# A Mamba-2 layer with a low-rank feed-forward: three convolutions moved ahead of a barrier, and the last tiles of the tail reordered

## What is computed

```python
proj = x_norm @ in_proj_w.T                  # 512 -> gate 8192, conv input 8192 + 2*8*128, dt 128
hBC  = silu(causal depthwise conv of 4 taps over the conv input + conv_b)
hs, Bm, Cm = hBC split into 128 heads x 64, 8 groups x 128, 8 groups x 128
dt = clip(softplus(dt + dt_bias), 0, 100);  A_dt = -exp(A_log) * dt, cumulated in chunks of 128 tokens
Y  = (C B^T * decay inside the chunk) @ (hs*dt) + C @ (state carried from earlier chunks) + hs * D
g  = Y * silu(gate), normed over each group of 1024 features, * norm_w
x  = x + g @ out_proj_w.T
h  = layernorm(x);  out = x + h @ W.T + b + sum over 16 experts of probs_e * (h @ A_e.T) @ B_e.T
```

## Time and profile before

| | us |
|---|---|
| median of 3 runs | 1635.05 (1633.94 to 1636.73) |
| the profiled execution | 1639.27 |
| its span, first to last instruction | 1637.5 |
| PE busy | 1598.2 |
| VectorE, ScalarE, GpSimd busy | 1261.2, 1147.9, 711.3 |
| mean granted clock of TensorE | 0.991 |

### The profile page before, as it was taken

The page is one execution under the profiler, slowest core; times in us unless marked ns, Lnnn a source line. Parts: engine busy times, 40 slices in busy tenths (PEclk is TensorE's granted clock), DMA queues, the critical chain, the costliest instruction groups (busy, mean ns, idle before and its releaser), DMA issues.

```text
span 1637.5 us, 26761 instructions
## 1 busy us (share of the span) xinstructions
PE 1598.2 (98%) x9616; PEld 1357.8 (83%) x9616; DVE 1261.2 (77%) x1974; ACT 1147.9 (70%) x2002; POOL 711.3 (43%) x543
## 2 busy tenths in 40 slices
PE   7799999999999999999999999999999999999997
PEld 4678888888888888888888888888888888888876
DVE  6577777887778787787778877787877877787776
ACT  5398668776777767876787766777678767777741
POOL 1145445354443543454453544435444444434542
PEclk9799999999999999999999999999999999999999
DMA  5533233323232332332333232233223323233211
GB/s 200 186 111 106 78 110 99 102 84 120 87 97 95 110 97 85 114 103 77 111 98 103 84 120 88 86 106 110 90 92 114 102 77 112 93 108 94 75 43 52
DMA packets 88244, 164.56 MB, mean 100 GB/s; under 512 B 23344, under 2 KB 39728, under 8 KB 87856
## 3 DMA queue, kind: packets, MB, share of 16 engines
q1 hardware_dynamic: 88112, 162.85, 30.5%
HBM read 157.03 MB, written 5.77 MB: 99 GB/s over the span
## 4 chain that ended last, share of the span: by engine, by line
PE 90%; issue 2%; DVE 2%; POOL 1%; ACT 1%; DVEq 0%; POOLq 0%; ACTq 0%
PE g_bank L714 9%; PE g_bank L715 8%; PE g_bank L716 8%; PE d_bank L733 7%; PE x_bank L714 7%; PE x_bank L715 7%; PE x_bank L716 7%; PE d_bank L773 3%; PE d_bank L775 3%; PE d_bank L774 3%; PE x_bank L773 3%; PE x_bank L774 3%; PE x_bank L775 3%; PE state_bank L722 2%; PE state_bank L740 2%; PE turn_bank L740 2%
## 5 line engine op out<-in xcount | busy, mean ns | idle before, releaser
L1294 POOL TENSOR_TENSOR w_low<-raw,w_high 128x512 fp32r<-128x512 f32 x141 | 182.3, 1293 | 580.2 <-ACT w_high L915 580.2
L1068 DVE SCALAR_TENSOR_TENSOR hs<-x_bank,cols,hs 128x1022 f32<-128x1022 f32 (+2 forms) x192 | 245.4, 1278 | 98.5 <-ACT hs L935 96.2
L925 ACT ACTIVATE scores<-scores,tables 128x128 f32<-128x128 f32 x1024 | 312.4, 392 | 0.0
L1308 POOL TENSOR_TENSOR y<-y,gate 128x512 f32<-128x512 f32 x128 | 188.7, 1494 | 205.5 <-DVE y L1130 205.5
L935 ACT ACTIVATE hs<-x_bank,cols 128x1024 f32<-128x1024 f32 x64 | 77.0, 1203 | 278.3 <-PE x_bank L716 278.3
L714 PE MATMUL g_bank<-x_high,w_high 128*128 128x512 f32 x624 | 251.2, 403 | 1.3 <-DVE bc L1147 1.3
L715 PE MATMUL g_bank<-x_low,w_high 128*128 128x512 f32 x624 | 244.0, 391 | 0.0
L716 PE MATMUL g_bank<-x_high,w_low 128*128 128x512 f32 x624 | 243.7, 391 | 0.0
L714 PE MATMUL x_bank<-x_high,w_high 128*128 128x512 f32 x512 | 199.6, 390 | 0.5 <-PEq L146 0.5
L716 PE MATMUL x_bank<-x_high,w_low 128*128 128x512 f32 x512 | 199.2, 389 | 0.0
L715 PE MATMUL x_bank<-x_low,w_high 128*128 128x512 f32 x512 | 199.2, 389 | 0.0
(11 more groups left out here) (185 smaller groups left out, 3492.2 us busy)
## 6 DMA issues: line engine op xcount, KB each, us to landing
scores<-sums_dram SPq DMA_DIRECT2D x128, 512.0 KB, 4.9
raw<-w_in SPq DMA_DIRECT2D x144, 256.0 KB, 2.9
grown_rows<-grown_dram SPq DMA_DIRECT2D x256, 96.0 KB, 2.8
out_raw<-w_out SPq DMA_DIRECT2D x64, 256.0 KB, 3.5
xt<-x SPq DMA_DIRECT2D x8, 256.0 KB, 5.6
mixed<-x SPq DMA_DIRECT2D x1, 2048.0 KB, 12.2
out<-mixed SPq DMA_DIRECT2D x8, 256.0 KB, 2.0
table_dram<-table SPq DMA_DIRECT2D x2, 768.0 KB, 3.2
```

The costliest lines, as they stand in the source:

```text
L925: op = s.activation(at, at, ACT.Relu, bias=col[:, r, c:c + 1], scale=-1.0)
L1068: v.scalar_tensor_tensor(out=hs[:, q % 2, :, i:], in0=x_bank[:, :, 0:SEQ - i], scalar=cols[:, q, TAPS - 1 - i:TAPS - i], in1=hs[:, q % 2, ...
L1294: pool.tensor_tensor(w_low[:, slot], raw[:, slot], w_high[:, slot].bitcast(F32), ALU.subtract)\
L1308: pool.tensor_tensor(y[:, b], y[:, b], gate[:, q % 2, b], ALU.mult).then_inc(y_ready, 1)
```

## The change

- In the prologue, PE projects B, C and now also the first x tile (into `head_bank`, `g_bank` and `x_bank`), straight after the dt product; the low-rank products come last, two banks by turns. ScalarE makes the first tap of all three and copies the six tables out of PSUM and the low-rank products to SBUF; VectorE makes the three other taps of all three and copies no table; GpSimd splits two more weight tiles and adds the low-rank products to the dense weight.
- SP loads `mixed` after the weight tiles, stores the dense weight last, and issues the loads of the first scores and growths ahead of the barrier. The load of the first tables waits for its own stores alone.
- Behind the barrier PE begins with the gate tile; B-C products go to `d_bank`; hs is turned between the two halves of the next x tile. ScalarE does the three silus first, and its differences (Relu) are split from its exponentials (`differences`, `decays`).
- In every unit, VectorE's `score` of sequence 0 comes ahead of the addition of output bank 3.
- In the tail, tile 8 is multiplied half by half (`out_part`), tile 9 after the sum of squares, the norm goes by pairs of tiles, the products use four banks and the splits three slots.

```diff
--- before.py
+++ after.py
...
-            sp.dma_start(mixed[:], x_tokens).then_inc(mixed_in, 16)
...
-            sp.wait_ge(dense_ready, KT)
-            sp.dma_start(dense_dram, dense[:].rearrange("p k d -> p (k d)")).then_inc(dense_stored, 16)
...
-                sp.dma_start(chunk_by_head[b], chunk_decay[:, b]).then_inc(stored[b], 16)
+                sp.dma_start(chunk_by_head[b], chunk_decay[:, b]).then_inc(tables_stored[b], 16)
+            for b in range(BATCH):
+                sp.wait_ge(sums_stored[b], 16)
+                sp.dma_start(scores[:, 0, b].rearrange("p r c l -> p (r c l)"),
+                             sums_dram[b * ALL].partition_broadcast(P)).then_inc(sums_in[0][b], 16)
+            for b in range(BATCH):
                 sp.wait_ge(table_ready, 3 * (b + 1))
                 sp.dma_start(table_dram[b].rearrange("p g n -> p (g n)"),
                              table[:, b].rearrange("p g k n -> p (g k n)"))\
-                  .then_inc(stored[b], 16)
+                  .then_inc(tables_stored[b], 16)
+            for b in range(BATCH):
+                sp.dma_start(scores[:, 1, b].rearrange("p r c l -> p (r c l)"),
+                             sums_dram[b * ALL + 1].partition_broadcast(P)).then_inc(sums_in[1][b], 16)
+            for b in range(BATCH):
+                sp.wait_ge(grown_stored[b], 16)
+                rows = grown_dram[b * ALL].rearrange("(r n) -> r n", r=PAIR)
+                for r in range(PAIR):
+                    sp.dma_start(grown_rows[r * HEAD_DIM:(r + 1) * HEAD_DIM, b].rearrange("p c l -> p (c l)"),
+                                 rows[r, P:].partition_broadcast(HEAD_DIM)).then_inc(grown_in[b], 16)
+            sp.wait_ge(dense_ready, KT)
+            sp.dma_start(dense_dram, dense[:].rearrange("p k d -> p (k d)")).then_inc(dense_stored, 16)
...
+            pool.wait_ge(wd_in, 16)
+            for k in range(KT):
+                pool.wait_ge(lora_out, k + 1)
+                pool.tensor_tensor(dense[:, k], dense[:, k], wd[:, k], ALU.add).then_inc(dense_ready, 1)
...
+                pe.wait_ge(bc_conv_ready, 1)
+                reached(pe, lora_out, k - 1)
...
+            for t in (0, 1):
+                for b in range(BATCH):
+                    project(t, b)
+            pe.wait_ge(z_ready, BATCH)
+            turn_table(0)
+            for b in range(BATCH):
+                project(2, b)
+            for i in range(1, 6):
+                turn_table(i)
             pe.wait_ge(lora_ready, ER)
             for k in range(KT):
                 lora(k)
-            pe.wait_ge(z_ready, BATCH)
-            project(0, 0)
-            project(0, 1)
-            turn_table(0)
-            turn_table(1)
-            project(1, 0)
-            for i in range(2, 6):
-                turn_table(i)
-            project(1, 1)
...
+            s.wait_ge(tap_bc_in, 16)
+            bc_tap0(0, head_bank[:])
+            high_part(3)
+            s.wait_ge(lora_in, 48)
+            for r in range(ER):
+                s.activation(lb[:, r], lb[:, r], ACT.Copy, scale=pr[:, r:r + 1]).then_inc(lora_ready, 1)
+            bc_tap0(1, g_bank[:])
+            high_part(4)
+            table_of(0)
+            growth(0)
+            growth(1)
+            for i in range(1, 6):
+                table_of(i)
+            s.wait_ge(cols_in[0], 16)
+            s.wait_ge(projected, BATCH * 3)
+            s.activation(hs[:, 0], x_bank[:], ACT.Identity, scale=cols[:, 0, TAPS - 1:TAPS],
+                         bias=cols[:, 0, TAPS:TAPS + 1]).then_inc(tap0_ready, 1)
+            for k in range(KT):
+                s.wait_ge(lora_product, k + 1)
+                s.activation(dense[:, k], head_bank[:, k % 2], ACT.Copy).then_inc(lora_out, 1)
+
         @block.vector
         def _(v):
             def stats_of(tb):
...
+                bc_tap(i, 0, head_bank)
+            for i in range(1, TAPS):
+                bc_tap(i, 1, g_bank)
+            for i in range(1, TAPS):
+                tap(i)
...
-            sp.wait_ge(dense_stored, 16)
-            for b in range(BATCH):
                 load_tables(0, b, 0)
-                load_sums(0, 0, b)
             load_weight(0, place(0, 2))
             load_out(0, 0)
-            for b in range(BATCH):
-                load_grown(0, b)
-            for b in range(BATCH):
-                load_sums(1, 1, b)
...
+            def out_part(j, c, i):
+                b, q, at = j % 2, flushed(j)[i], slice(c * P, (c + 1) * P)
+                pe.matmul(out_bank[c], y_high[:, q, b, at], out_high[:, q], start=(i == 0), stop=False)
+                pe.matmul(out_bank[c], y_high[:, q, b, at], out_low[:, q], start=False, stop=False)
+                return pe.matmul(out_bank[c], y_low[:, q, b, at], out_high[:, q], start=False, stop=(i == 1))
...
+                if tb in (2, 3):
+                    pe.wait_ge(added, emptied(ALL + 1, tb - 2))
+                if tb >= len(product_bank):
+                    pe.wait_ge(ready, tb + 1 - len(product_bank))
...
+                            if k == 0 and b == 0:
+                                pe.wait_ge(b_tok_ready, 1)
+                                turn_hs(0, 0, 0)
+                                turn_hs(0, 0, 1)
...
-            pe.wait_ge(bc_conv_ready, 1)
+            pe.wait_ge(bc_conv_ready, 2)
             for b in range(BATCH):
-                project(0, 0, b, x_bank[:, b])
+                project(0, 1, b, g_bank[:, b])
...
+                bc_of(b, d_bank)
 
             over_groups(pe, body)
-            later_outs(UNITS + 1, ALL + 1)
+            later_outs(UNITS - 1, ALL - 1)
+
+            pe.wait_ge(out_low_ready, ALL)
+            for c in range(CHUNKS):
+                pe.wait_ge(added, emptied(ALL - 1, c))
+                out_part(UNITS, c, 0)
+            pe.wait_ge(y_low_ready, ALL)
+            for c in range(CHUNKS):
+                out_part(UNITS, c, 1).then_inc(out_done, 1)
+            pe.wait_ge(square_added, (UNITS - 1) * GROUPS)
+            var_of()
+            for c in range(CHUNKS):
+                pe.wait_ge(added, emptied(ALL, c))
+                out_product(UNITS + 1, c)
 
...
-            high_part(0, 1)
-            s.wait_ge(projected, BATCH * 2)
-            s.activation(bc_conv[:, 1], g_bank[:], ACT.Identity, scale=tap_bc[:, 1, TAPS - 1:TAPS],
-                         bias=tap_bc[:, 1, TAPS:TAPS + 1]).then_inc(bc_tap0_ready, 1)
-            high_part(0, 2)
             silu_bc(0, 0)
+            silu_bc(0, 1)
+            silu_hs(0, 0)
+            high_part(0, 3)
+            differences(0, 0, 0, 0)
+            keep_b(0, heads)
             for b in range(BATCH):
+                silu_gate(0, 0, 0, b)
+            differences(0, 0, 0, 1)
+            for b in range(BATCH):
+                decays(0, 0, b)
+            for b in range(BATCH):
+                s.wait_ge(sums_stored[b], 16)
+                s.wait_ge(grown_stored[b], 16)
                 s.wait_ge(tables_stored[b], TABLE_STORES)
             s.wait_ge(dense_stored, 16)
-            keep_b(0, d_bank)
-            tap0(0, 0, 0)
-            high_part(0, 3)
-            silu_bc(0, 1)
-            silu_hs(0, 0)
-            for b in range(BATCH):
-                silu_gate(0, 0, 0, b)
-            for b in range(BATCH):
-                decays(0, 0, 0, b)
...
-            norm_std(0)
             for tb in range(TB):
-                if tb == 3:
-                    norm_std(1)
+                if tb % 2 == 0:
+                    norm_std(tb // 2)
                 s.wait_ge(xt_turned, tb + 1)
-                if tb >= 2:
-                    s.wait_ge(product, tb - 1)
-                s.activation(xt_high[:, tb % 2].rearrange("p k t -> p (k t)"), xn_bank[tb % 2], ACT.Copy)\
+                if tb >= SPLIT:
+                    s.wait_ge(product, tb + 1 - SPLIT)
...
+                    scores_here = last or j not in (5, 6)
+                    if scores_here:
+                        score(g, j, k, 0)
                     if k > 2:
                         add_outs(g, j - 1, (3,))
-                    if last or j not in (5, 6):
-                        for b in range(BATCH):
-                            score(g, j, k, b)
+                    if scores_here:
+                        score(g, j, k, 1)
...
-            for at in range(CHUNKS):
-                normed_out(GROUPS, at)
+
+            def summed(pair):
+                for tb in (2 * pair, 2 * pair + 1):
+                    normed_out(GROUPS, tb)
+
+            summed(0)
             norm_stats(0)
-            norm_stats_end(0)
+            norm_moments(0)
+            summed(1)
+            norm_rstd(0)
             normed(0)
             normed(1)
-            add_outs(GROUPS - 1, UNITS + 1, range(CHUNKS))
-            for at in range(CHUNKS, TB):
-                normed_out(GROUPS, at)
+            norm_stats(1)
             low_of(0)
+            norm_moments(1)
             low_of(1)
+            norm_rstd(1)
             normed(2)
```

(36 more changed lines are left out.)

276 lines of the change are left out of this document (126 added, 150 removed).

## The result

The changed kernel takes **1619.43 us** (median, 1618.50 to 1619.84), the kernel before on the same chip 1635.89 (1633.94 to 1637.21): a ratio of 0.990, 95% interval 0.9887 to 0.9912. That is 16.5 us by the medians, where 22.1 were forecast. The time lies in the range, 6.4 us above the forecast of 1613.0. The profiled execution took 1619.32 (span 1617.6), so this one stands at its median, while the one of before stood 3.4 above the median of 1635.89. Between the two profiled spans lie 19.9 us. In the later comparisons the kernel before had medians of 1636.7 to 1637.9. The changed kernel has no second time of its own; its nearest variants, runs 3 and 4, took 1619.0 and 1618.9 beside 1636.85, so the gain is 16.5 to 18 us.

The account below looks back on a forecast made before the run. PE was taken as the bound, busy 98% of the span with a full middle, so only the ends give time: 14.2 at the start plus 7.9 at the end, 22.1 off 1635.05, gives 1613.0 us; range 1608.5 to 1621.

Parts of the forecast that it names:

- R1: Rival, start: PE's clock falls under lora and at the barrier, tables come late; start gives 9.9, time 1617; chance 0.20.
- R2: Rival, tail: VectorE's sums double beside GpSimd's bias additions, first product at half clock; end gives 3.3, time 1617.5; chance 0.12.
- The 14.2: Start: PE reaches the gate projection of unit 1 at 76.5 in place of 90.70, 14.2 us earlier.
- 58.3: End of the prologue: the barrier falls at about 58.3 us, 1.8 later than before.
- Unseen 1: At the barrier: PE's clock may fall behind a 2.5 us gap; taken as none, 1.9 at the bad end.
- Unseen 2: Behind the barrier: first table load queues behind the dense store; worst 1.2 late, 0.4 past cover; taken as nothing.
- 7.9: Tail: 6.8 earlier, plus 1.9 for a full clock, less 0.8 for VectorE late twice; 7.9 us gained.
- (a): VectorE's score of batch 0 ahead of the fourth output addition: worth 0.6 at unit 63, nothing elsewhere.
- (b): Tail: tile 8 by halves, the half with unit 62 filling PE's wait for y_low; worth 0.6.
- (c): Tail: norm by pairs of tiles, first product 6.8 earlier, PE's gap 1.4 instead of 4.98, clock staying full.
- R3: Rival, middle units: the score swap makes scores end late under GpSimd's work, kernel slower, 1640 at 0.45 per unit; chance 0.03.
- R4: Rival, first units: the freed time turns into waits paced by ScalarE, no gain, 1635; chance 0.03.

Follow-up runs that it names:

- run 3: Changed kernel with VectorE's fourth output addition put back ahead of both scores (no swap): 1619.02 us, ratio to the kernel before 0.9888.
- run 4: Changed kernel plus eleven products that nobody reads, keeping PE busy up to the barrier: 1618.89 us, ratio to the kernel before 0.9886.
- run 1: The kernel before, unchanged, profiled once more: ratio 1.0004; the profiled execution took 1635.38 us.
- run 5: Changed kernel with GpSimd's two later weight splits (tiles 3 and 4) held until VectorE has both sums: 1616.38 us, ratio to the kernel before 0.9879.
- run 9: Changed kernel, y_low of unit 62 behind unit 63's states, additions of banks 2 and 3 ahead of the last y_low: 1617.53 us, ratio 0.9880.
- run 6: Changed kernel with ScalarE's six table copies written contiguously, table entries permuted: 1619.26 us, ratio to the kernel before 0.9896.
- run 2: Kernel before with only the new tail (halves, pairs) and the score swap, old start: 1629.71 us, ratio to the kernel before 0.9955.
- run 7: Changed kernel with the six table copies made by VectorE between its taps instead of ScalarE: 1622.94 us, ratio to the kernel before 0.9920.
- run 8: Changed kernel with VectorE's y_low of unit 62 moved behind the states of unit 63: 1618.78 us, ratio to the kernel before 0.9891.
- run 10: Changed kernel with the edits of run 5 and run 9 together: 1615.14 us, ratio to the kernel before 0.9869.
- run 11: The kernel of run 10 plus products that nobody reads, keeping PE busy up to the barrier: 1614.75 us, ratio to the kernel before 0.9859.

## Why the forecast was right in kind and too good in size

The measured 1619.43 lies in the whole range of 1608.5 to 1621, but above the forecast's own 1609 to 1616.5 and above what R1 or R2 alone would give (1617, 1617.5). It is inside by the bad end alone.

**The step that failed first** is the sentence "I subtract from both". The forecast compared its steps with one profiled execution of before, took the 4.2 us over the median for something that the changed kernel would share, and took it off the sum again. It was not shared. In run 1 the gate of unit 1 is 3.9 earlier and the span 3.8 shorter: 2.3 of it by the end of the dt product, which came early in the changed kernel too, and 1.6 in the very stretch that the change rebuilds. Another part was no excess at all, as later medians of before lie 1.7 to 2.8 us over the 1635.05 that the forecast had. The 14.2 was worked out against 90.70, where 86.80 and 87.08 also occur; nothing let it stand beside a subtraction of the whole 4.2. Of the miss of 6.4 us, 4.2 are this step and 2.2 the terms: 1.4 at the start and 0.7 at the end.

**The rows.** The forecast says that the high waits, 5.0 and 4.6, are all of the end, and puts the 4.6 at unit 63. Its rows don't place them: 1.5 of the 4.6 were at unit 0. The view's highest wait, 9.2 for the normed tiles at the very start, it passes over. A turn with 0.45 to the next instruction took 0.35 at the place named (1612.29 to 1612.64). None of the three moves the sum by more than 0.2.

**Barrier, "58.3".** Right (PE at 58.60, the first issue of SyncE behind it at 58.41), but the working was wrong twice, with errors that cancelled. VectorE had the dt product 1.6 earlier (26.2, not 27.8: the clock had risen sooner), and lost 2.2 us in its two groups to GpSimd's moved splits, (2.39 - 1.29) + (2.42 - 1.36). The forecast priced the splits' move at nothing and had R2's rule only for the tail. The Trainium skill ("SBUF — State Buffer", "Who interferes with whom") says that a VectorE instruction with two SBUF inputs contends with a GpSimd one that reads SBUF; runs 3, 5 and 9 agree. The table copies took 0.98, near the 1.05 taken. By the Trainium skill's rule that each access that crosses to a new 16-byte line pays a penalty ("SBUF — State Buffer", "Door 1: The DMA port swizzle") ScalarE pays for the pattern; the 0.98 with it and the 0.53 of a contiguous copy in run 6 (1.05 for two) agree. The other half of the step, a barrier 1.2 earlier without the pattern, is near the 1.0 of run 6, but was worth no time.

**Behind the barrier.** Unseen 1, the clock, taken as none "because 2.5 is nearer 1.88": the gap was 2.95, and the fall came, for 1.6 of its 1.9. PE's turns of B started at 65.76, where B+5.8 gives 64.1. From there to the gate PE gained 0.3 on the forecast, and 1.4 stayed. Unseen 2, the late tables, came with 1.19, its worst value, and cost nothing more only because PE was late by the clock anyway; in run 4, with a full clock, they did cost. Both had been put side by side as separate bad ends; together they cost the larger, not the sum. The rest of the schedule is right within that 0.3: from the B-C products to the gate of unit 1 it said 11.8 and took 11.5.

**End, "7.9".** 7.2 in the profile, and the same in run 2. The 0.7 that lacks is all in the last stretch, 29.7 from the first product in place of 28.9, and it is its two waits. As idle time they are 0.69 and 0.33, but from start to start, which is what PE loses, they cost 1.5 in place of 0.8: from turn 5 to product 4 pass 1.30 where 0.36 is usual, and from product 4's last matmul to turn 6 0.72 where 0.23 is. Of the 0.7 more, 0.5 is the last pair of sums (1.91 for 1.40), which stands right ahead of the low part of product 4. Part (a), the swap at 0.6, gave its 0.6 and kept 0.4 (run 3). Parts (b) and (c) stood: the gap of 4.98 became 1.13, the first product runs at full clock, product 4 waits 0.69 (0.2 foretold) and turn 6 0.33 (0.6 foretold).

**Rivals.** Of R1's three parts two came, the clock at the barrier and the tables; under lora the clock did not fall (granted 1.00 from 44 to 56 us in the changed kernel, as in its variants of the table below but run 7, where PE waited up to 1.4 for each copy). R2 came as 0.5 in the last pair of sums, which PE paid at product 4. That pair took 0.95 a sum, over the 0.75 that the forecast gave as a sign of being wrong; run 9, with both sums of the first pair stretched, shows that more of it was near. R3 failed as the middle is full, 1400.00 of 1400.00, and no longer than before. R4 failed with at least 8.9 at the start.

**Still open:** why the tables' load takes 5.9 us (the share of 1.01 points to the queues in front of it; no run gave it a free path), what sets whether the clock falls behind a wait of 2.96, and how much of the 3.0 us of run 5 is the splits and how much the clock.

## What to carry to other kernels

A forecast against one profiled execution should ask where that execution differs from the median, above all in stretches with waits and a changing clock, before its excess is taken off the sum. An instruction moved on an engine that is not the bound still takes its load on SBUF with it: look at what VectorE does at the new place, in a prologue as well as in a tail. When two costs end in the same wait, mending one shows the other; both engines' lines have to be moved before the time follows.

## What was not expected of the hardware

The clock behind the wait at the barrier had three outcomes. Ten executions, of the changed kernel and its variants, with the wait, the mean granted clock of 58 to 64 us (62.1 to 68.1 in run 7, whose barrier is later), and the time from PE's first matmul behind the barrier to its B-C products (24 matmuls and six transposes, the same in all):

| execution | wait | clock | us |
|---|---|---|---|
| runs 5, 8 | 2.96 | 1.00 | 6.2 |
| the changed kernel, runs 3, 7, 9 | 2.95 to 2.96 | 0.72 | 7.8 |
| runs 6, 10 | 2.96 to 2.97 | 0.50 | 9.1 |
| runs 4, 11 (filled) | 0.45 to 0.46 | 1.00 | 6.2 |

Runs 5 and 10 are the same program up to there. So a wait near 3 us cost nothing, 1.6 or 2.9 us here, by the execution, and the filled one cost nothing in two. A shorter wait behaved so too: behind the 1.13 ahead of the first product of the norm the clock stayed full in the changed kernel and in runs 9 and 11, and fell in run 10 (0.50 from 1587 to 1589 us), for 1.4 us. The start itself differs too: PE passes the barrier at 57.85 in run 3 and at 59.45 in run 8, with the same program ahead of it and 32.2 us from VectorE's second z in both.

VectorE's two-operand instructions on SBUF took 1.8 to 2.0 times as long beside GpSimd's (2.42 for 1.36, 2.28 for 1.27, 2.87 for 1.42), and GpSimd's own went from 1.27 (3.80 for three) to 1.54. VectorE's instructions that read PSUM took 0.69 in the tail beside GpSimd as without it.
